# Mixed blocks of four experts in TensorE column groups, in a decoder layer with a mixture of experts

## The chip, the cores and the metric

One core of one Trainium2 chip runs the whole program in one launch. The metric is the device time of that launch in microseconds. The profile is one execution of the same program, taken by the hardware profiler.

## The reference

A decoder layer on 16 sequences of 256 tokens with 256 features, all in float32: self-attention with an altered score function, cross-attention in chunks of 64, and a feed-forward part, each followed by an addition and a layer norm. The change is in the feed-forward part, a mixture of 32 experts with 4 experts per token and a shared expert. Cut to this:

```python
def _L0_ffn_ref(hidden_states, router_weight, router_bias, gate_w, up_w, down_w, shared_gate_w, shared_up_w, shared_down_w):
    tokens = hidden_states.reshape(-1, H)                 # 4096 x 256
    topk_idx, topk_w = _route(tokens, router_weight, router_bias)   # 4 of 32 experts
    gate_vals = jax.nn.silu(jnp.einsum('th,eih->tei', tokens, gate_w))
    up_vals = jnp.einsum('th,eih->tei', tokens, up_w)
    hidden_vals = gate_vals * up_vals                     # 128 wide per expert
    expert_out = jnp.einsum('tei,ehi->teh', hidden_vals, down_w)
    sel = jnp.take_along_axis(expert_out, topk_idx[:, :, None], axis=1)
    mixed = (sel * topk_w[:, :, None].astype(sel.dtype)).sum(1)
    ...
    return mixed + shared
x = _layernorm(x + _L0_ffn_ref(x, L0_ffn_router_weight, L0_ffn_router_bias, L0_ffn_gate_w, L0_ffn_up_w, L0_ffn_down_w, L0_ffn_shared_gate_w, L0_ffn_shared_up_w, L0_ffn_shared_down_w), axis=-1)
```

## The kernel before

The program has three stages. In the first one a loop over the sequences computes both attentions, the router and the shared expert's inner values; GpSimd scatters each token's row (256 features, its routing weight and its address, 258 words) into the DRAM tensor `routed`, in which each expert has a region of its own. That makes 4096 x 4 = 16384 rows. Meanwhile SyncE loads the 32 experts' weights into `w_expert`, where all of them stay.

Then `vec_tables` (L1100) and `pe_tables` (L509) turn the counts of the experts into tables. Each expert has as many blocks of 128 rows as it needs, the last of them partly filled; `shapes` (L45) fixes the number of blocks at the most that any counts can need, (16384 + 32 x 127) // 128 = 159. For each block the tables hold its row address (`tab_i[0]`), the place of its expert's weights in `w_expert` (`tab_i[1]`), and `away`, which sends rows behind an expert's last one to a place where nobody reads. The row addresses are released by the semaphore `v_adr`, the weights' places by `v_tab`.

The second stage, the expert stage, runs over the 159 blocks. In the text a slot is one block's turn. For slot n:

- SyncE loads 128 rows of `routed` into `rowsb` (L1372), 16 buffers deep; from slot 16 on it first waits for the store of slot n - 16 (`st_y`). All loads stand in one queue. After slot 16's it also issues the load of `hs_sb`, 4096 KB, for the last stage (L1375).
- PE transposes the rows (`pe_xbT`, L526, its matmuls are at L284), ScalarE copies the result into `xbT` (L724).
- ScalarE copies the expert's gate and up weights into one of four buffers `wgu` (L857), because a matmul's weights are read from a place that is fixed in the program.
- PE computes gate and up (`pe_gu`, L533 to L540): four matmuls with 128 weight columns from `wgu` and 128 moving columns from `xbT`.
- ScalarE takes the tanh (L853), VectorE makes the inner values `hb` (L1129, L1132).
- PE computes the down projection (`pe_down`, L542 to L546): `hb` as weights, 256 moving columns read from `w_expert` at a register's address.
- VectorE combines it with the routing weight and the row (L1144) into one of four buffers `yb`, so that it waits for the store of slot n - 4, and makes the addresses (L1137); GpSimd scatters the result into the DRAM tensor `y` (L1293).

The order is written out by hand. PE's turn of slot n is transpose for n + 3, gate and up for n + 2, down for n; a float32 matmul shows as two records in the trace. Registers are filled eight at a time by a table load (`values`, L268), one for each eight blocks on PE, ScalarE and SyncE.

The third stage gathers four rows of `y` for each token, adds the shared expert's part on PE and applies the last layer norm (`sync_out` L561 and what follows it). Its code is not touched.

## Time and profile before

| | us |
|---|---|
| median of 3 runs | 827.7 |
| lowest and highest run | 824.57, 830.9 |
| profiled execution, from first to last instruction (span) | 830.3 |
| PE busy | 765.2 |
| VectorE, ScalarE, GpSimd busy | 581.5, 494.4, 368.0 |

The page gives no separate time for the profiled execution. Busy time is a mean over the three stages; the stages lie at about 13 to 503 us, 503 to 764 us and 764 to 830 us of the span. All times in views count from the span's start.

### The profile page before, as it was taken

The numbers are of one execution on the slowest core, as the hardware profiler recorded it, in microseconds if no ns is written. First come the engines' busy times: TensorE is split into PE (matmuls) and PEld (weight loads), VectorE is DVE, ScalarE is ACT, GpSimd is POOL, SyncE is SP. The second block draws the span as 40 slices with busy tenths as digits, with TensorE's granted clock in tenths as the row PEclk, the third lists the DMA queues.
The fourth block names the chain that finished last, engine by engine and source line by source line (L and its number), as shares of the span: only waits on it lengthen the run. The fifth ranks groups of instructions, "written<-read, shape, count | busy, mean of one in ns | idle before, by whom it ended". The sixth has DMA issues, their size and how long they took to land.

```text
span 830.3 us, 21803 instructions
## 1 busy us (share of the span) xinstructions
PE 765.2 (92%) x8308; PEld 665.4 (80%) x8308; DVE 581.5 (70%) x2094; ACT 494.4 (60%) x1166; POOL 368.0 (44%) x437
## 2 busy tenths in 40 slices
PE   7969899999999999999997756799999999999986
PEld 6758788888888888888876636799999999998554
DVE  2345487898889888898888763366666666665486
ACT  0546666767767767777654414467676766764143
POOL 0101214334543355334554662366666666665142
PEclk9999999999999999999989877799999999999999
DMA  6582221332433334332113436755555555552996
GB/s 233 156 214 84 84 84 53 108 118 92 142 121 110 120 99 129 120 110 89 66 65 103 142 111 189 270 172 167 177 172 173 171 169 170 176 168 83 370 401 241
DMA packets 69642, 124.95 MB, mean 150 GB/s; under 512 B 9665, under 2 KB 43329, under 8 KB 69282
## 3 DMA queue, kind: packets, MB, share of 16 engines
q1 hardware_dynamic: 51394, 81.60, 32.1%
q0 software_dynamic: 13776, 37.77, 12.6%
q10 hardware_dynamic: 4368, 4.20, 1.4%
q8 instruction: 66, 1.08, 0.6%
q14 instruction: 38, 0.31, 0.1%
HBM read 73.16 MB, written 50.36 MB: 149 GB/s over the span
## 4 chain that ended last, share of the span: by engine, by line
PE 78%; DMA 7%; DVE 6%; SPq 5%; issue 2%; POOL 1%; ACT 1%; ACTq 0%; DVEq 0%
PE banks L538 17%; PE banks L284 10%; PE banks L545 8%; PE banks L386 3%; PE banks L377 3%; PE banks L354 3%; PE banks L322 3%; PE banks L367 3%; PE banks L489 3%; SPq L567 3%; PE banks L331 3%; PE banks L463 3%; PE banks L498 3%; PE banks L339 3%; DMA w_expert_tile<-y 2%; PE banks L429 2%
## 5 line engine op out<-in xcount | busy, mean ns | idle before, releaser
L1293 POOL DMA_INDIRECT y<-yb_tile,idcol_tile x159 | 152.4, 959 | 112.9 <-DVE yb_tile L1144 110.2
L538 PE MATMUL banks<-xbT_tile,wgu_tile 128*128 128x128 f32 x1272 | 172.0, 280 | 0.0
L538 PEld LDWEIGHTS banks<-xbT_tile,wgu_tile 128*128 128x128 f32 x1272 | 158.6, 196 | 0.1
L1144 DVE SCALAR_TENSOR_TENSOR yb_tile<-banks,rowsb_tile 128x256 f32<-128x256 f32 x159 | 76.9, 484 | 84.2 <-PE banks L545 76.1
L857 ACT ACTIVATE wgu_tile<-w_expert_tile 128x512 f32 x159 | 98.9, 622 | 11.8 <-DVE tab_i_tile L1121 11.8
L545 PE MATMUL banks<-w_expert_tile,hb_tile 128*128 x318 | 96.3, 385 | 5.2 <-DVE hb_tile L1132 5.2
L1271 POOL DMA_INDIRECT routed<-row_tile,idx_tile x64 | 62.5, 976 | 68.8 <-PE banks L399 53.2
L853 ACT ACTIVATE gb_tile<-banks 128x128 f32<-128x128 f32 x159 | 44.1, 277 | 79.1 <-PE banks L538 79.1
L1265 POOL DMA_INDIRECT routed<-row_tile,idx_tile x64 | 61.7, 964 | 31.1 <-issue 18.5
L1246 POOL TENSOR_TENSOR rs_tile<-ve_tile,half_neg_tile 128x2 f32<-128x2 f32 x16 | 11.1, 693 | 143.6 <-DVE ve_tile L960 143.6
L284 PE MATMUL banks<-const_tile,rowsb_tile 128*128 128x128 f32 x318 | 62.2, 278 | 7.1 <-DMA rowsb_tile<-routed 7.1
L724 ACT ACTIVATE xbT_tile<-banks 128x256 f32<-128x256 f32 x159 | 59.7, 376 | 13.2 <-PE banks L284 12.9
L284 PEld LDWEIGHTS banks<-const_tile,rowsb_tile 128*128 128x128 f32 x318 | 45.4, 144 | 23.7 <-DMA rowsb_tile<-routed 7.9
L545 PEld LDWEIGHTS banks<-w_expert_tile,hb_tile 128*128 128x128 f32 x318 | 48.8, 194 | 6.4 <-issue 6.4
L1132 DVE TENSOR_TENSOR hb_tile<-hb_tile,banks 128x128 f32<-128x128 f32 x159 | 45.7, 287 | 5.5
L1241 POOL TENSOR_TENSOR xc_tile<-x_sb_tile,c_out_tile 128x256 f32<-128x256 f32 x32 | 22.7, 734 | 55.9 <-ACT x_tile L816 28.4
L1129 DVE SCALAR_TENSOR_TENSOR hb_tile<-gb_tile,banks 128x128 f32<-128x128 f32 x159 | 44.6, 281 | 3.8 <-ACT gb_tile L853 3.8
L638 ACT ACTIVATE w_expert_tile<-w_expert_tile,fnmr_tile,frs_tile 128x256 f32<-128x256 f32 x32 | 17.6, 593 | 48.5 <-DVE fnmr_tile L618 48.5
L631 POOL TENSOR_TENSOR frs_tile<-fve_tile,fhalf_tile 128x2 f32<-128x2 f32 (+1 forms) x17 | 17.9, 1056 | 42.6 <-DVE fve_tile L613 42.6
L322 PE MATMUL banks<-xT_tile,g_qk_tile 128*128 128x256 f32 x128 | 32.4, 399 | 4.5 <-DMA xT_tile<-xT 4.5
L498 PE MATMUL banks<-x2T_tile,w_shared_in_tile 128*128 128x256 f32 x128 | 33.5, 409 | 1.3 <-ACT sc_tile L836 1.2
L595 PE MATMUL banks<-w_expert_tile,const_tile 128*128 128x512 f32 (+1 forms) x68 | 30.1, 575 | 3.7 <-DMA w_expert_tile<-y 3.6
(206 smaller groups left out, 1784.4 us busy)
## 6 DMA issues: line engine op xcount, KB each, us to landing
rowsb_tile<-routed SPq DMA_DIRECT2D x159, 129.0 KB, 2.2
w_expert_tile<-y SPq DMA_DIRECT2D x15, 1024.0 KB, 15.0
w_expert_tile<-w_expert SPq DMA_DIRECT2D x16, 768.0 KB, 4.6
cT_tile<-ctxT SPq DMA_DIRECT2D x16, 384.0 KB, 3.2
routed<-zrow_tile SPq DMA_DIRECT2D x1, 4128.0 KB, 22.5
xT_tile<-xT SPq DMA_DIRECT2D x16, 256.0 KB, 3.0
x_sb_tile<-x SPq DMA_DIRECT2D x16, 256.0 KB, 2.7
inner<-hs_tile SPq DMA_DIRECT2D x16, 256.0 KB, 2.3
```

Source lines behind the costliest of these rows:

```text
L284: return e.transpose(o, i, ident)
L322: m = e.matmul(bank[5][:, db * S:(db + 1) * S], g_qk[:, k, db * P:(db + 1) * P], xT[:, k, :], start=k == 0, stop=k == DK - 1)
L498: m = e.matmul(bank[7][:, b * S:(b + 1) * S], w_shared_in[:, k, 2 * P + b * P:3 * P + b * P], x2T[i % 2][:, k, :], start=k == 0, stop=k == ...
L538: m = e.matmul(bank[2 + u % 4][:, h * P:(h + 1) * P], wgu[u % WG][:, k * D + h * EI:k * D + (h + 1) * EI], xbT[u % 2][:, k * P:(k + 1) * P ...
L545: e.matmul(bank[6 + u % 2][:, 0:D], hb[u % 4][:, :], w_flat[:, bass.ds(w + 2 * D, D)], start=True, stop=True).then_inc(SEM["p_down"], 1)
L724: e.activation(o, i, ACT.Copy).then_inc(SEM[done], 1)
L857: e.activation(wgu[u % WG][:, :], w_flat[:, bass.ds(w, DK * D)], ACT.Copy)
L1132: e.tensor_tensor(hb[u % 4][:, :], hb1[u % 2][:, :], bank[2 + u % 4][:, EI:2 * EI], ALU.mult)\
L1144: e.scalar_tensor_tensor(yb[n % YS][:, :], bank[6 + u % 2][:, 0:D], rowsb[n % ROWS][:, D:D + 1], rowsb[n % ROWS][:, 0:D], ALU.mult, ALU.ad ...
L1265: e.indirect_dma_start(routed, bass.IndirectOffsetOnAxis(ap=idx[i % 2][:, 0, k:k + 1], axis=0), row[i % 2][:, k, 0, :], None).then_inc(SEM ...
L1271: e.indirect_dma_start(routed, bass.IndirectOffsetOnAxis(ap=idx[i % 2][:, 1, k:k + 1], axis=0), row[i % 2][:, k, 1, :], None).then_inc(SEM ...
L1293: e.indirect_dma_start(y, bass.IndirectOffsetOnAxis(ap=idcol[n % ROWS][:, :], axis=0), yb[n % YS][:, :], None).then_inc(SEM[f"st_y{n % YS} ...
```

## The change

The 16384 rows are exactly 128 full blocks. After the change there are 128 whole slots ("F") and 12 mixed ones ("Q"). A mixed slot has four parts of 32 rows, each of an expert of its own. An expert's remainder, what is left behind its full blocks, is either given a whole slot (`F`) or cut into one to four parts of 32 rows. The tables rank the experts by the number of parts of their remainders, and the largest remainders get the whole slots that are left. `quarters` finds the largest number of parts that any counts can leave, so that 12 mixed slots are enough. `slots` puts one mixed slot behind every ten whole ones and the last eight whole ones at the end.

In a mixed slot the roles of the operands are swapped: `xbT` is the weights, 32 columns for each part, and the experts' weights are the moving operand, 256 columns, each part writing the 32 partitions of its own column group. The inner values come out with the rows on the partitions, so PE transposes `hb` (`pe_hbT`), ScalarE copies it (`act_hbT`), and the down projection is four matmuls again. The weights of the four experts are read from `wq`, which SyncE fills for each mixed slot from DRAM with four DMAs; it is laid over `w_cross` and `w_shared_in`, which are not used any more in this stage. ScalarE's copy into `wgu` falls away for a mixed slot. The rows of a mixed slot come in four loads of 32 rows.

```diff
+QR = P // 4
+LAG = 6
 def shapes(nseq):
     n = nseq * S
-    blocks = (n * TOPK + E * (P - 1)) // P
-    return n, P + n, blocks
+    full = n * TOPK // P
+    groups = -(-quarters(n * TOPK, full) // 8) * 2
+    return n, P + n, full, groups
+def slots(nseq):
+    _, _, full, groups = shapes(nseq)
+    every = full // groups
+    out = []
+    for g in range(groups):
+        out += [("F", g * every + j) for j in range(every)] + [("Q", g)]
+    return out + [("F", j) for j in range(groups * every, full)]
...
-        w_cross = sb("w_cross", [P, DK, 4, D])
+        w_early = sb("w_early", [P, DK * 4 * D + DK * 2 * SH])
+        w_cross = w_early[:, 0:DK * 4 * D].rearrange("p (k j n) -> p k j n", k=DK, j=4)
+        w_shared_in = w_early[:, DK * 4 * D:].rearrange("p (k n) -> p k n", k=DK)
+        wq = w_early[:, :].rearrange("p (q n) -> p q n", q=4)
...
+        def pe_gu(e, s):
+            e.wait_ge(SEM["a_xbT"], s + 1)
+            kind, g = SLOTS[s]
+            o = bank[2 + s % 4]
...
+            if kind == "Q":
+                e.wait_ge(SEM["ld_wq"], 64 * (g + 1))
+            for k in range(DK if kind == "Q" else 0):
+                for q in range(4):
+                    at = k * P + q * QR
+                    m = e.matmul(o[q * QR:(q + 1) * QR, 0:2 * EI], xbT[s % 2][:, at:at + QR],
+                                 wq[:, q, k * D:(k + 1) * D], start=k == 0, stop=k == DK - 1)
             m.then_inc(SEM["p_gu"], 1)
+        def pe_hbT(e, s):
+            e.wait_ge(SEM["v_hb"], s + 1)
+            transpose(e, bank[2 + s % 4][:, 2 * EI:2 * EI + P], hb[s % 4][:, :]).then_inc(SEM["p_hbT"], 1)
+        def pe_down(e, s, w):
...
+                e.wait_ge(SEM["a_hbT"], g + 1)
+                for q in range(4):
+                    m = e.matmul(o[q * QR:(q + 1) * QR, 0:D], hbT[g % 2][:, q * QR:(q + 1) * QR],
+                                 wq[:, q, 2 * D:3 * D], start=True, stop=True)
...
+        def act_hbT(e, s):
+            g = SLOTS[s][1]
+            e.wait_ge(SEM["p_hbT"], g + 1)
+            copy(e, hbT[g % 2][:, :], bank[2 + s % 4][:, 2 * EI:2 * EI + P], "a_hbT")
...
         def vec_tables(e, ch):
-            ch(e.tensor_scalar(cnt_i[:, :], counts[:, :], float(P - 1), None, ALU.add))
+            ch(e.tensor_scalar(cnt_i[:, :], c("round", E), counts[:, 0:1], None, ALU.add))
+            e.tensor_scalar(cnt_i[:, 0:2], cnt_i[:, 0:2], 7, None, ALU.logical_shift_right)
+            ch(e.tensor_scalar(cnt_i[:, 2:3], cnt_i[:, 2:3], 5, None, ALU.logical_shift_right))
...
+            ch(e.tensor_scalar(above[:, :], bank[7][0:E, 8:8 + E], order[:, 0:1], None, ALU.is_gt))
+            ch(e.tensor_reduce(rank[:, :], above[:, :], AX.X, ALU.add))
...
+            def load_wq(g):
+                if g % 2 == 0:
+                    wanted.update(values(mybir.EngineType.SP, 1, FULL + 4 * g))
+                if g > 0:
+                    e.wait_ge(SEM["p_down"], SLOTS.index(("Q", g - 1)) + 1)
+                for q, a in enumerate(quarter(g)):
+                    e.dma_start(wq[:, q, :], d["w_expert"].rearrange("p e n -> p (e n)")[:, bass.ds(wanted.pop(a), 3 * D)])                        .then_inc(SEM["ld_wq"], 16)
...
+            for s, (kind, n) in enumerate(SLOTS):
+                if s >= ROWS:
+                    e.wait_ge(SEM[f"st_y{s % YS}"], 16 * ((s - ROWS) // YS + 1))
...
+                if s >= LAG and SLOTS[s - LAG][0] == "Q":
+                    load_wq(SLOTS[s - LAG][1])
+                if s == ROWS:
                     e.wait_ge(SEM["st_hs"], 16 * nseq)
                     e.dma_start(hs_sb[:, :, :, :].rearrange("p i k s -> p (i k s)"), inner[:, :]).then_inc(SEM["ld_hs"], 16)
```

Two places show what moves. The first is PE, in the slots around a mixed one. Before, every turn reads as these rows do (L284 transposes a slot's rows, L538 is gate and up, L545 the down projection; "waits" names the semaphores):

```order
L284 MATMUL banks<-const_tile,rowsb4_tile 128x128 [waits ld_row4]
L284 MATMUL banks<-const_tile,rowsb4_tile 128x128
L538 MATMUL banks<-xbT1_tile,wgu3_tile 128x128 [waits a_xbT]
L538 MATMUL banks<-xbT1_tile,wgu3_tile 128x128 x3
L545 ISA [waits v_hb]
L545 MATMUL banks<-w_expert_tile,hb1_tile 128x256
```

After the change these stand around the first mixed slot, number 10 (L338 transposes, L600 and L620 are gate and up and down of a whole slot, L607 and L624 those of a mixed one):

```order
L607 MATMUL banks<-w_early_tile,xbT0_tile 32x256 [waits ld_wq,a_xbT]
L607 MATMUL banks<-w_early_tile,xbT0_tile 32x256 x7
L620 ISA [waits v_hb]
L620 MATMUL banks<-w_expert_tile,hb0_tile 128x256
L338 MATMUL banks<-const_tile,rowsb12_tile 128x128 [waits ld_row12]
L338 MATMUL banks<-const_tile,rowsb12_tile 128x128
L600 MATMUL banks<-xbT1_tile,wgu3_tile 128x128 [waits a_xbT]
L600 MATMUL banks<-xbT1_tile,wgu3_tile 128x128 x3
L338 MATMUL banks<-const_tile,hb2_tile 128x128 [waits v_hb]
L620 ISA [waits v_hb]
L620 MATMUL banks<-w_expert_tile,hb1_tile 128x256
```

The four gate and up matmuls of one slot have become eight with a wait for the weights' load, and the transpose of `hb` (hb2 is slot 10's) stands ahead of the down projection of slot 9.

The second place is SyncE's queue. Before, one row load follows the other, each behind the store of the slot 16 before it:

```order
L1372 ISA [waits st_y2]
L1372 DMA rowsb14_tile<-routed 128x258
L1372 ISA [waits st_y3]
L1372 DMA rowsb15_tile<-routed 128x258
L270 TENSOR_LOAD tab_i_tile
L1372 ISA [waits st_y0]
L1372 DMA rowsb0_tile<-routed 128x258
```

After the change the load of slot 27 (rowsb11) is followed by the fetches for the second mixed slot, number 21:

```order
L1489 ISA [waits st_y3]
L1489 DMA rowsb11_tile<-routed 128x258
L1478 REGISTER_ALU [waits p_down]
L1478 DMA w_early_tile<-w_expert 128x768
L1478 REGISTER_ALU
L1478 DMA w_early_tile<-w_expert 128x768
L1478 REGISTER_ALU
L1478 DMA w_early_tile<-w_expert 128x768
L1478 REGISTER_ALU
L1478 DMA w_early_tile<-w_expert 128x768
L1489 ISA [waits st_y0]
```

The fetches stand behind a row load that waits for the store of slot 11, and the next row load stands behind them.

## Rows read from the trace of the kernel before

**Rows 1.** The page: PE in 40 slices of the span, tenths; the DMA packets.
```profile
PE   7969899999999999999997756799999999999986
...
DMA packets 69642, 124.95 MB, mean 150 GB/s; under 512 B 9665, under 2 KB 43329, under 8 KB 69282
```

**Rows 2.** Stretches: length, busy PE, PEld, DVE, ACT, POOL (instructions), PE clock, DMA share, GB/s.
```profile
60.00:430.00 370.00, 361.89 (x5313) 317.24 (x5311) 303.66 (x1022) 260.83 (x568) 149.22 (x199) 1.00 0.31 99
...
545.00:763.00 218.00, 217.37 (x1683) 202.82 (x1682) 146.32 (x565) 148.91 (x418) 135.44 (x142) 1.00 0.55 165
...
532.00:536.00 4.00, 4.00 (x19) 3.71 (x18) 1.90 (x8) 1.56 (x4) 1.72 (x3) 0.50 0.53 177
```

**Rows 3.** Groups by line, 420 to 780 us: busy us, mean ns, idle before.
```profile
L538 PE MATMUL banks<-xbT_tile,wgu_tile 128*128 128x128 f32 x1272 | 172.0, 280 | 0.0
...
L545 PE MATMUL banks<-w_expert_tile,hb_tile 128*128 x318 | 96.3, 385 | 5.2 <-DVE hb_tile L1132 5.2
```

**Rows 4.** Timeline of PE in the steady part: start us, duration us, engine, line.
```profile
559.86 0.60 PE L545 MATMUL banks<-w_expert_tile,hb_tile 128*128 x2
560.29 0.38 PE L284 MATMUL banks<-const_tile,rowsb_tile 128*128 128x128 f32 x2
560.51 1.06 PE L538 MATMUL banks<-xbT_tile,wgu_tile 128*128 128x128 f32 x8
561.40 0.60 PE L545 MATMUL banks<-w_expert_tile,hb_tile 128*128 x2
...
756.18 0.60 PE L545 MATMUL banks<-w_expert_tile,hb_tile 128*128 x2
```

**Rows 5.** Timeline of PE, matmuls in column groups of the attention stage and their successor.
```profile
256.44 0.65 PE L443 MATMUL banks<-sha_tile,vM_tile 128*32 128x64 f32 x32
...
257.36 1.10 PE L455 MATMUL banks<-rden_tile,const_tile 128*32 128x64 f32 x64
258.39 1.99 PE L386 MATMUL banks<-w_expert_tile,w_cross_tile 128*128 128x256 f32 x8
```

**Rows 6.** Timeline of DVE, the same beat as rows 4.
```profile
562.82 0.29 DVE L1132 TENSOR_TENSOR hb_tile<-hb_tile,banks 128x128 f32<-128x128 f32 x1
```

**Rows 7.** Timeline, start of the expert stage: scatter 0, gate and up 4, load 16.
```profile
512.18 0.95 POOL L1293 DMA_INDIRECT y<-yb_tile,idcol_tile  x1 [12.09 <-DVE yb_tile L1144]
...
512.98 1.06 PE L538 MATMUL banks<-xbT_tile,wgu_tile 128*128 128x128 f32 x8
...
514.72 0.33 SPq L1372 DMA_DIRECT2D rowsb_tile<-routed  x1
```

**Rows 8.** Timeline around the load of hs_sb; in brackets the idle time before.
```profile
516.81 0.96 POOL L1293 DMA_INDIRECT y<-yb_tile,idcol_tile  x1 [0.59 <-DVE yb_tile L1144]
...
529.37 0.48 DVE L1144 SCALAR_TENSOR_TENSOR yb_tile<-banks,rowsb_tile 128x256 f32<-128x256 f32 x1 [3.86 <-DMA y<-yb_tile,idcol_tile]
...
530.58 1.22 PE L545 MATMUL banks<-w_expert_tile,hb_tile 128*128 x2 [2.27 <-DVE hb_tile L1132]
```

**Rows 9.** DMA issues: KB each, median us from issue to landing.
```profile
rowsb_tile<-routed SPq DMA_DIRECT2D x159, 129.0 KB, 2.2
...
w_expert_tile<-w_expert SPq DMA_DIRECT2D x16, 768.0 KB, 4.6
...
hs_sb_tile<-inner SPq DMA_DIRECT2D x1, 4096.0 KB, 14.4
```

**Rows 10.** Timeline of SyncE's queue: the first 16 row loads; two of them.
```profile
502.69 8.68 SPq L1372 DMA_DIRECT2D rowsb_tile<-routed  x16
...
507.94 0.85 SPq L1372 DMA_DIRECT2D rowsb_tile<-routed  x2
```

**Rows 11.** Timeline of the tables; the last line is of the chain that ended last.
```profile
490.73 0.20 PE L513 MATMUL banks<-const_tile,macc_tile 128*32 128x1 f32 x2 [1.34 <-DVE hs_tile L1071]
...
496.64 0.24 DVE L1120 TENSOR_SCALAR tab_i_tile<-tab_tile 1x160 int32<-1x160 f32 x1
...
499.13 2.54 DMA routed<-row_tile,idx_tile
```

More of the change, by code:

```diff
@@ L4 @@
 from contextlib import ExitStack
+import functools
 P = 128
@@ L65, in constants @@
         (p[:, None] <= np.arange(E)[None]),
-        np.tile(np.arange(table), (P, 1)),
+        row(np.arange(full), np.arange(4 * groups)),
         p[:, None],
-        n * TOPK + np.arange(blocks)[None, :] * P + p[:, None],
+        p[:, None] % QR,
+        -p[:, None],
+        row([0, P - 1, QR - 1]),
+        n * TOPK + np.arange(full + groups)[None, :] * P + p[:, None],
     ]
     at, out = 0, {}
-    for name, a in zip(("ident", "before", "ones", "headmask", "denmask", "spread", "region", "upto", "blockno", "part", "nowhere"), parts):
+    for name, a in zip(("ident", "before", "ones", "headmask", "denmask", "spread", "region", "upto", "number",
+                        "part", "part32", "minus", "round", "nowhere"), parts):
         out[name] = (at, a.shape[1])
@@ L220, in build @@
         ctx_a.close()
+        place = sb("place", [E, E + 3])
+        over = sb("over", [E, 1])
+        order = sb("order", [E, 1])
+        above = sb("above", [E, E])
+        rank = sb("rank", [E, 1])
+        some = sb("some", [E, 1])
+        rows_full = sb("rows_full", [E, 1])
+        step = sb("step", [1, TABLE])
         past = sb("past", [E, TABLE])
@@ L263, in __call__, with quarter, loads @@
                 self.e.wait_ge(SEM[self.name], self.n)
[L265 to L266 removed]
         def values(engine, row, n):
             _, v = nc.values_load_multi_w_load_instructions(
[L271 removed]
+                tab_i[0:1, row, n:n + UNROLL], engines=[engine], min_val=0,
+                max_val=(E * REGION - (P if n < FULL else QR), (E - 1) * 3 * D)[row],
                 skip_runtime_bounds_check_because="the table is clamped to the experts and their regions for any counts")
             return {n + u: v[u] for u in range(UNROLL)}
+        def quarter(g):
+            return range(FULL + 4 * g, FULL + 4 * g + 4)
+        def loads(s):
+            return sum(64 if SLOTS[a][0] == "Q" else 16 for a in range(s % ROWS, s + 1, ROWS))
         blk = ctx.enter_context(nc.Block())
```

299 lines of the change are left out of this document (170 added, 129 removed).

## The prediction

> **What bounds the kernel now.** I read the page first: TensorE stands at 9 tenths in nearly every slice [rows 1]. The change touches the expert stage, so the stretches come next: from 545 to 763 us PE is busy 217.37 of 218.00 us at a granted clock of 1.00, DVE 146, ACT 149, POOL 135, and the DMA share is 0.55 [rows 2]. The groups by line name the work there: 159 slots, each with 8 records of L538 and 2 of L545 on PE [rows 3], besides two transposes (L284). The timeline shows the beat: the down projections at 559.86 and 756.18 are 127 slots apart, 1.546 us each, and within a slot the transposes (0.22 to the next line), gate and up (0.89) and down (0.44) follow each other without a gap [rows 4]. So a slot costs PE's own time, and a slot removed is worth 1.546 us as long as nothing else takes PE's place.
>
> Two places are different. The stage begins only when the rows are there, and around 520 to 537 the 4096 KB load of hs_sb, which takes 14.4 us [rows 9], holds back the scatters: the one issued at 516.81 lands when the combine at 529.37 starts, PE waits 2.27 us for hb, and the granted clock reads 0.50 [rows 2, 8]. The change keeps this stall, so it is no term of the sum.
>
> **What goes.** 159 slots become 140, in the pattern ten whole, one mixed, twelve times, then eight whole. 19 x 1.546 = 29.4 us of PE time leave the bounding engine. DVE and POOL lose their 19 as well and stay below PE.
>
> **What a mixed slot adds on PE.** Gate and up are 8 matmuls of 32 weight columns by 256 moving columns in four column groups, down is 4 such. Whether four groups run at once, rows show: L443 does 32 matmuls of 32 columns by 64 (64 records) between 256.44 and 257.36, L455 the same number between 257.36 and 258.39 [rows 5]. The steady slot gives the price of moving columns: 0.44 us for the one 256-column matmul of down [rows 4], hence 0.11 per 64 columns, and 32 of these one after the other would take 3.5 us. They took 0.92 and 1.03, 3.8 and 3.4 times less. So the mixed slot's gate and up take about 2 x 0.44 = 0.88 and down 0.44, the same as a whole slot's. Beyond that: (a) the transpose of hb, half of the 0.22 for two, 0.11; (b) entering and leaving the column groups. If the groups ran at a full four times the speed, L455 would take 0.88; it takes 0.15 more and L443 0.04 more; I take 0.18 for each of the two grouped stretches of a mixed slot, 0.36, a little above both, since here each stretch is entered from whole matmuls and left again; (c) the transpose stands ahead of the down projection of the slot before and waits for hb of the mixed slot. In the steady beat hb is written at 562.82 plus 0.29 = 563.11, and the down projection of the slot before begins at 561.40 + 1.546 = 562.95 [rows 4, 6]: 0.16 us of wait, behind which the down projection queues. The ScalarE copy of the transposed hb has a whole slot until down wants it, and ScalarE saves its weight copy for a mixed slot. Sum 0.62, times 12 = 7.4 us. Lower bound 0.11 (all else hidden), upper bound 2.0, if each of the four changes between whole and grouped matmuls cost as much as an isolated matmul lasts (385 ns, L545 in [rows 3]) and the wait is 0.4.
>
> The Trainium skill speaks against the change here. "TensorEngine Tiling (Array Packing)", Key Properties, says that a change of tiling mode drains the array, and "TensorE: Matmul & The Clock Gate", Single matmul latency, gives a constant of 398 cycles at 2.4 GHz; an estimate from the two is 0.17 us a drain, four to a mixed slot, 0.66 where I have 0.36, some 4 us more in all. The rows above hold the two lines L443 and L455 behind each other without that.
>
> **What a mixed slot adds on the queues.** Its weights are fetched from DRAM for each mixed slot: four DMAs of 384 KB into w_early, 1536 KB, 12 times. SP issues them behind the row load of six slots later, which itself waits for the store of the slot ten before the mixed one. So their time is short and can be counted. In the trace the row load number 16 goes out at 514.72, when store 0 has landed; the gate-and-up matmuls of slot 4 start at 512.98, so those of slot 10, the first mixed one, would start at 512.98 + 6 x 1.546 = 522.26 [rows 7]. That leaves 7.5 us. All later groups repeat this: the same ten slots stand between. Against it: 0.52 us for the row load (two in 0.85 with 0.33 for the last), and a table load for every second group. Its price: 16 row loads took 8.68 us, 15 x 0.52 + 0.33 = 8.13, the rest, 0.55, is the one table load; 0.28 on average [rows 7, 10]. The transfer: 129 KB land in 2.2 us and 768 KB in 4.6 us [rows 9], 3.76 ns more per KB, so 1536 KB land 2.2 + 1407 x 0.00376 = 7.5 us after the first issue. Together 8.3 us, 0.8 us too late. PE then stands at the mixed slot's gate and up, and down, scatter and combine of the slots behind queue up: the whole 0.8 us is lost, 12 x 0.8 = 9.6 us. Bounds: the 4096 KB load needs (14.4 - 2.2) / 3967 = 3.1 ns per KB, landing in 6.5 us, no wait; and if the scatters' half of the 0.55 DMA share [rows 2] comes on top of that price, it is 2.2 + 5.3 / 0.73 = 9.5 us, a wait of 2.8. I take 0.8, because the 768 KB loads were timed beside traffic of 0.31 DMA share (60 to 430 us in [rows 2]), about what the scatters make.
>
> Do the fetches hold back the scatters as hs_sb does? A combine comes 4 slots, 6.2 us, after the one whose store it waits for. A scatter issued at 512.18 has landed at 514.72, 2.5 us [rows 7], and the combine itself is 0.48 [rows 8]. That leaves about 3 us. The hs_sb load is made of large packets (only 360 of the 69642 are 8 KB or more [rows 1]), these of 3 KB: if each of a scatter's 1 KB packets stands behind one of 3 KB, it moves four times the bytes of its own, and a landing grows by some 1.2 us. Hidden. The row loads queued behind a fetch are wanted ten slots later. The first fetch comes ahead of hs_sb, and the hs_sb stall moves back with it; I keep its size.
>
> **The tables.** Between PE's L513 (490.73) and v_adr (L1120, 496.64 + 0.24) 15 DVE operations turn into 29, with a fourth hand-over to PE and three more matmuls. The 15 with three hand-overs took 6.15 us, 0.41 each, so 14 more take at most 5.7; at the 0.24 that L1120 itself takes they are 3.4. I take 4, since most of the new ones are one column wide, so v_adr comes near 500.9. The row loads wait for the last scatter anyway, issued at 499.13 and landed 2.54 later at 501.67 [rows 11]. Cost 0, at most 0.9 by the first price. Table loads on PE and ScalarE stand between other waits and cost nothing now; ScalarE's now precede the copy that uses them, and ScalarE, busy 149 of 218 us, waits for gate and up in every slot, which covers that.
>
> **Sum.** 29.4 - 7.4 - 9.6 - 0 = 12.4 us less. The profiled execution's span is 830.3 us; the page states no separate time for it, and the span is 2.6 above the median of the runs shown (827.7) and within their 824.57 to 830.9. From 830.3 it goes to 817.9, and against the median to 815.3, which I predict.
>
> **The rivals.**
> A, the fetches are in time. Speaks for it: the 4096 KB load's 3.1 ns per KB. Against: the 3.76 of the smaller ones. 29.4 - 7.4 = 22.0, 805.7 us.
> B, the other side: the fetch is the bound of every group. Place: PE before the mixed slot's gate and up. Break-even is a wait of (29.4 - 7.4) / 12 = 1.8 us; from there the kernel is slower. At 2.8 us it is 33.6 + 7.4 - 29.4 = 11.6 slower, 839.3 us. For it: the scatters share the engines, and PE's wait stands in each group anew. If the wait reaches the 2.3 us of [rows 8], the half clock beside it can follow too; four us at 0.50, as one window there shows [rows 2], lose 2 us more in each group, 24 in all. Against it: the price of 9.5 us for a fetch charges the scatters twice, as said above.
> C, the column groups don't overlap with 256 moving columns: 12 matmuls x 0.44 instead of 3 x 0.44, 4.0 us a mixed slot, 48 us, 863 us. For it: nothing in the trace has 256 columns in a group. Against: L443 and L455, with four different moving operands and with one.
> The Trainium skill ("TensorE: Matmul & The Clock Gate", Measured speedup vs the span model) gives 3.07 for four row tiles and 2.38 for three column tiles; by the first, an estimate, 1.32 us of grouped work become 1.72, 4.8 us in all, still the forecast's case.
>
> **How the numbers follow.** Forecast (wait 0.3 to 1.6) 0.45; A 0.25; B 0.22; C 0.08. Low end: A with mixed slots at 0.4 instead of 0.62, 803. High end: B, 839. More than 1% (8.3 us, about what a measurement of this kernel can tell from no change) faster: A, and the forecast up to a wait of 1.1, 0.28: 0.53. Slower by over 1%: C, and B from a wait of 2.5, 0.14: 0.22. The rest, 0.25, is within 1%.
>
> **What would show it.** A whole slot stays at 1.546; a mixed slot without its wait is 0.6 longer; PE's idle time before the grouped matmuls of gate and up, released by the w_early DMA, is near 0.8 times 12; the four fetches land 7.5 us after the first issue; the granted clock stays 1.00 between 545 us and the end of the stage; the first row load stays near 502.7. Wrong would be a wait of nothing or above 1.8, combines waiting for stores at every group, or grouped records that follow each other 0.44 us apart.

## The result

The changed kernel takes 837.17 us, median of 5 runs (834.13 to 841.48), against 828.52 (824.57 to 831.67) for the kernel before on the same chip: a ratio of 1.0107 with a 95% interval of 1.0068 to 1.0145. Two later controls with both kernels unaltered, where the kernel before is as fast, gave 833.71 against 827.20 and 833.22 against 827.64. The prediction was 815.3, faster; the kernel is about 1% slower. The value lies in the stated range of 803 to 839. A slower kernel was given 30 chances in 100 (rivals B and C), one slower by over 1% 22. The ratios leave out executions in a slower state of the chip: none here, three in the experiments (842.21, 1000.2 and 4368.72 us).

The profiled execution has a span of 834.7 us and a time of 836.51.

This is the page of the kernel after, to be held against [rows 1]: PE in 40 slices of the span, the granted clock of PE (TensorE) in tenths, the DMA packets.

```profile
PE   7879999999999999999987638989898889799987
...
PEclk9989999999999999999999769999999999999999
...
DMA packets 73482, 138.83 MB, mean 166 GB/s; under 512 B 10401, under 2 KB 41633, under 8 KB 73122
```

PE's slices of the expert stage alternate between 8 and 9 where they all stood at 9: something recurs. Here are the windows of the kernel after, with the columns of [rows 2]:

```profile
506.00:545.00 39.00, 31.55 (x236) 27.25 (x234) 19.48 (x76) 20.28 (x56) 18.21 (x19) 0.96 0.88 317
545.00:763.00 218.00, 196.29 (x1567) 167.22 (x1568) 119.91 (x464) 126.57 (x350) 110.68 (x116) 0.98 0.66 210
577.84:586.34 8.50, 6.55 (x51) 5.93 (x50) 5.16 (x20) 4.79 (x14) 4.49 (x6) 1.00 0.91 301
```

From 545 to 763 us PE is busy 196.29 us where it was 217.37. It has less to do, as meant, but the 21 us are now idle time inside the stage. The groups by line of the kernel after say what it waits for (busy us, mean ns, idle time before and its releaser; they answer to [rows 3]):

```profile
L600 PE MATMUL banks<-xbT_tile,wgu_tile 128*128 128x128 f32 x1024 | 137.8, 278 | 0.0
...
L620 PE MATMUL banks<-w_expert_tile,hb_tile 128*128 x256 | 80.4, 397 | 1.9 <-DVE hb_tile L1238 1.9
...
L607 PE MATMUL banks<-w_early_tile,xbT_tile 128*32 128x256 f32 x192 | 15.5, 445 | 27.3 <-DMA w_early_tile<-w_expert 27.3
...
L1251 DVE SCALAR_TENSOR_TENSOR yb_tile<-banks,rowsb_tile 128x256 f32<-128x256 f32 x140 | 67.7, 484 | 114.6 <-PE banks L620 86.3 <-DMA y<-yb_tile,idcol_tile 20.8 <-PE banks L624 7.6
```

The first matmul of the mixed slots' gate and up waits 27.3 us in all for the weights, 2.27 for each of the 12; the forecast was 9.6 in all, 0.8 for each. And the combines wait 20.8 us in all for a store, where the kernel before has 8.1.

This is the timeline of PE around one mixed slot in the kernel after (it answers to [rows 4]):

```profile
582.03 0.60 PE L620 MATMUL banks<-w_expert_tile,hb_tile 128*128 x2
...
583.57 0.60 PE L620 MATMUL banks<-w_expert_tile,hb_tile 128*128 x2
584.01 0.38 PE L338 MATMUL banks<-const_tile,rowsb_tile 128*128 128x128 f32 x2
586.34 1.07 PE L607 MATMUL banks<-w_early_tile,xbT_tile 128*32 128x256 f32 x16 [1.96 <-DMA w_early_tile<-w_expert]
587.35 0.70 PE L620 MATMUL banks<-w_expert_tile,hb_tile 128*128 x2
587.88 0.38 PE L338 MATMUL banks<-const_tile,rowsb_tile 128*128 128x128 f32 x2
588.10 1.06 PE L600 MATMUL banks<-xbT_tile,wgu_tile 128*128 128x128 f32 x8
589.21 0.33 PE L338 MATMUL banks<-const_tile,hb_tile 128*128 128x128 f32 x1
589.37 0.62 PE L620 MATMUL banks<-w_expert_tile,hb_tile 128*128 x2
589.83 0.38 PE L338 MATMUL banks<-const_tile,rowsb_tile 128*128 128x128 f32 x2
590.05 1.06 PE L600 MATMUL banks<-xbT_tile,wgu_tile 128*128 128x128 f32 x8
591.04 0.64 PE L624 MATMUL banks<-w_early_tile,hbT_tile 128*32 128x256 f32 x8
```

The whole slots are still 1.54 us apart (582.03, 583.57). The 16 records of L607 with 256 moving columns take 1.07 us to their last end and 1.01 to the next line. One after the other they would take eight times 0.44 us: the four column groups do run at once. These are SyncE's queue in the same stretch, and the landing of the last of the four fetches, from the chain that ended last:

```profile
577.28 0.34 SPq L1489 DMA_DIRECT2D rowsb_tile<-routed  x1
577.84 2.21 SPq L1478 DMA_DIRECT2D w_early_tile<-w_expert  x4
```

```profile
579.71 6.50 DMA w_early_tile<-w_expert
```

The row load that the fetch stands behind goes out at 577.28, the first fetch at 577.84, the last lands at 586.21. The third window above is just this stretch: the 16 DMA engines are busy 0.91 of the time and move 301 GB/s. The DMA issues of the kernel after are these (KB each, median us from issue to landing; they answer to [rows 9]):

```profile
w_early_tile<-w_expert SPq DMA_DIRECT2D x48, 384.0 KB, 5.1
rowsb_tile<-routed SPq DMA_DIRECT2D x128, 129.0 KB, 2.6
...
hs_sb_tile<-inner SPq DMA_DIRECT2D x1, 4096.0 KB, 18.3
...
y<-yb_tile,idcol_tile POOLq DMA_INDIRECT x140, 3.3
```

A store lands after 3.3 us at the median, where it took 2.5 in the kernel before. Beside a fetch it is worse. These are a scatter and a combine of the kernel after, around the fetch issued at 619.24:

```profile
619.26 0.96 POOL L1398 DMA_INDIRECT y<-yb_tile,idcol_tile  x1 [0.59 <-DVE yb_tile L1251]
```

```profile
626.15 0.48 DVE L1251 SCALAR_TENSOR_TENSOR yb_tile<-banks,rowsb_tile 128x256 f32<-128x256 f32 x1 [1.95 <-DMA y<-yb_tile,idcol_tile]
```

The combines between them start at 620.05, 621.59 and 623.14. So the one at 626.15 is the fourth behind the one whose scatter went out at 619.26, and takes the same `yb` buffer: that scatter took 6.9 us until its buffer was used again.

### The profile page after: what moved, and what is told of

The parts are those of the page before. It is cut to its first block, busy times and chain, and to the rows that moved or that the text cites. A ratio compares the mean times of both kernels' runs of the same rounds, so it can differ in the third digit from the quotient of the medians.

```text
span 834.7 us, 21727 instructions
## 1 busy us (share of the span) xinstructions
PE 745.9 (89%) x8274; PEld 629.4 (75%) x8274; DVE 564.1 (68%) x2036; ACT 475.6 (57%) x1109; POOL 349.7 (42%) x418
## 4 chain that ended last, share of the span: by engine, by line
PE 62%; DMA 19%; DVE 8%; SPq 6%; issue 3%; POOL 1%; ACT 1%; ACTq 0%; DVEq 0%
DMA w_early_tile<-w_expert 8%; PE banks L338 8%; DMA y<-yb_tile,idcol_tile 6%; PE banks L600 5%; PE banks L440 3%; PE banks L431 3%; PE banks L408 3%; PE banks L376 3%; PE banks L421 3%; PE banks L620 3%; PE banks L543 3%; PE banks L385 3%; PE banks L517 3%; PE banks L552 3%; PE banks L393 3%
## 5 line engine op out<-in xcount | busy, mean ns | idle before, releaser
L1398 POOL DMA_INDIRECT y<-yb_tile,idcol_tile x140 | 134.1, 958 | 141.1 <-DVE yb_tile L1251 138.6
L1251 DVE SCALAR_TENSOR_TENSOR yb_tile<-banks,rowsb_tile 128x256 f32<-128x256 f32 x140 | 67.7, 484 | 114.6 <-PE banks L620 86.3
L600 PE MATMUL banks<-xbT_tile,wgu_tile 128*128 128x128 f32 x1024 | 137.8, 278 | 0.0
L600 PEld LDWEIGHTS banks<-xbT_tile,wgu_tile 128*128 128x128 f32 x1024 | 127.4, 196 | 0.2
L944 ACT ACTIVATE wgu_tile<-w_expert_tile 128x512 f32 x128 | 79.8, 623 | 22.4 <-DVE tab_i_tile L1226 15.6
L620 PE MATMUL banks<-w_expert_tile,hb_tile 128*128 x256 | 80.4, 397 | 1.9 <-DVE hb_tile L1238 1.9
L805 ACT ACTIVATE xbT_tile<-banks 128x256 f32<-128x256 f32 x140 | 52.7, 377 | 14.0 <-PE banks L338 11.9
L338 PE MATMUL banks<-const_tile,rowsb_tile 128*128 128x128 f32 x280 | 56.0, 283 | 3.3 <-DMA rowsb_tile<-routed 3.2
L338 PEld LDWEIGHTS banks<-const_tile,rowsb_tile 128*128 128x128 f32 x280 | 39.0, 145 | 22.9 <-issue 7.1
L620 PEld LDWEIGHTS banks<-w_expert_tile,hb_tile 128*128 128x128 f32 x256 | 39.5, 195 | 9.3 <-issue 9.3
L607 PE MATMUL banks<-w_early_tile,xbT_tile 128*32 128x256 f32 x192 | 15.5, 445 | 27.3 <-DMA w_early_tile<-w_expert 27.3
```

Source lines behind the costliest of these rows:

```text
L338: return e.transpose(o, i, ident)
L600: m = e.matmul(o[:, h * P:(h + 1) * P], wgu[s % WG][:, k * D + h * EI:k * D + (h + 1) * EI], xbT[s % 2][:, k * P:(k + 1) * P], start=k == ...
L620: m = e.matmul(o[:, 0:D], hb[s % 4][:, :], w_flat[:, bass.ds(w.pop(g) + 2 * D, D)], start=True, stop=True)
L805: e.activation(o, i, ACT.Copy).then_inc(SEM[done], 1)
L944: e.activation(wgu[s % WG][:, :], w_flat[:, bass.ds(w.pop(n), DK * D)], ACT.Copy)
L1251: e.scalar_tensor_tensor(yb[s % YS][:, :], bank[6 + s % 2][:, 0:D], rowsb[s % ROWS][:, D:D + 1], rowsb[s % ROWS][:, 0:D], ALU.mult, ALU.ad ...
```

## The experiments

There are three theories. **L**, lateness: each fetch lands too late and PE's wait stands in full; the cure is to start the fetch earlier. **S**, the fetches hold the scatters back, so the combines run late; the cure is more `yb` buffers or less traffic. **M**, the mixed slot itself costs PE more than thought. Sixteen runs in four groups test them, each group beside the kernel before on its own chip. The chips are of two kinds: on those of groups 1 and 3 the kernel before takes 870 and 871 us instead of 828, so only ratios are compared between the two kinds. A ratio with its interval is not the quotient of the two medians, and can differ from it by up to 0.5%.

`LAG` is the number of slots by which a fetch's place in SyncE's queue lies behind the mixed slot's own row load. A smaller one is an earlier fetch. Below 6, the first fetch needs a wait of its own for the tables, in all these kernels:

```diff
-LAG = 6
+LAG = 5        # 4 in other runs
...
+                if g == 0:
+                    e.wait_ge(SEM["v_tab"], 1)
```

**Group 1 (kernel before 870.12 us).**

Fetch one slot earlier:

> The changed kernel with the fetches for a mixed slot issued one slot earlier (LAG 5; SyncE also waits for v_tab before the first). Theory L (lateness): the loss is PE's wait for fetches that go out too late; the wait falls from 27 us in all to 8 to 12, and the time by about 16 to 20 us from the changed kernel's 837, so 817 to 821. Rival S (stores): the 18 MB of fetches hold back the scatters, and what PE no longer waits for the fetch it waits through the combines; the time stays above 830 and the combines' wait for stores grows above 25 us.

Measured 846.26 us, 0.9709 (0.9682 to 0.9737). The fetch waits are gone, a mean of 0.06 us for each mixed slot, where 8 to 12 us in all were expected to stay. The combines wait 26.2 us for stores, as S expects, and the kernel is faster all the same.

Fetch two slots earlier:

> The changed kernel with the fetches two slots earlier (LAG 4), as early as the buffer of the mixed slot before is free. Theory L: PE waits for a fetch less than 3 us in all, 808 to 814 us, the granted clock is 1.00 after 545 us. Rival S: combines wait more than 25 us for stores, 825 us or more. Theory M (mixed slots themselves cost much more than 0.62 us over a whole one): the waits are gone and the time is still near 825, with PE busy.

Measured 843.84 us, 0.9686 (0.9665 to 0.9707), no fetch waits; the combines wait 24.9 us for stores.

Only the first fetch is issued, and all mixed slots use its weights, so eleven fetches are left out. `LAG` stays 6:

```diff
-                e.wait_ge(SEM["ld_wq"], 64 * (g + 1))
+                e.wait_ge(SEM["ld_wq"], 64)
...
-                if s >= LAG and SLOTS[s - LAG][0] == "Q":
+                if s >= LAG and SLOTS[s - LAG] == ("Q", 0):
```

> The changed kernel with the fetch for the first mixed slot only; the 11 others use the same weights again, so the output of the experts' remainders is left wrong, and 16.5 MB of traffic are left out. What remains is the price of 140 slots: with 0.9 us for a mixed slot over a whole one 29.4 - 10.8 = 18.6 us below before, and up to 5 more for a shorter stall at the load of hs_sb: 804 to 811 us. Against the kernel with LAG 4: L expects a difference below 4 us, S above 10 us.

Measured 839.35 us, 0.9646 (0.9630 to 0.9662). Against LAG = 4 the combines' waits for stores fall from 24.9 to 6.3 us, and the time by 4.5 us, although this kernel still waits 2.9 us for its one fetch. That lies between what L (below 4) and S (above 10) expected: fetches that arrive early still cost something, but little.

Six `yb` buffers, paid for with four of the sixteen row buffers, and fetches as early as the queue allows:

```diff
-ROWS = 16
-YS = 4
+ROWS = 12
+YS = 6
...
-LAG = 6
+LAG = 0
```

> Fetches as early as with LAG 4, but six buffers yb instead of four and twelve row buffers instead of sixteen (LAG 0 puts the fetch behind the same store). A combine waits for the store six slots back. L: as LAG 4 except for the stall at the load of hs_sb, 3 us shorter for the two more slots of slack, 805 to 811 us. S: more than 10 us below LAG 4, and combines no longer wait for stores outside 510 to 540 us.

Measured 849.75 us, 0.9757 (0.9741 to 0.9773). No combine waits for a store, yet it is 6 us slower than LAG = 4 alone. PE waits for rows instead, 13.7 us, 9.9 of them in one piece; LAG = 4 has 2.0. I read this as twelve row buffers being too few to cover the 4096 KB load of `hs_sb`. What the store waits of the combines cost is less than what these buffers cost.

All four ratios are better than the forecast's own (815.3 of 827.7, 0.985), and the changed kernel had not run on such a chip. So group 2 has the controls.

**Group 2 (kernel before 827.39 us).** These are the controls, both kernels unaltered:

> The kernel before, unchanged, as a control: the chip of the last four runs gave 870 us for it where the first gave 828. Ratio 1.00. If the chip is the slow one again, its profile shows where the 42 us lie. Theory S for that chip: scatters land later than the 6.2 us that four buffers allow, combines wait for stores in most slots, and a whole slot takes about 1.7 us or more. Rival: the attention stage is longer and the slot stays 1.546.

> The changed kernel, unchanged, as a control on the same chip. On a chip where before takes 828: 837. On one where it takes 870: theory L expects it 25 to 30 us above the kernel with LAG 4 (0.969 of before), so a ratio of 0.995 to 1.005; S expects no more than 5 us above it.

Measured 827.20 (1.0009, 0.9978 to 1.0040) and 833.71 (1.0074, 1.0040 to 1.0109). The result holds; the fetch waits are 20.6 us.

The kernel before with six `yb` and twelve row buffers:

> The kernel before with six buffers yb and twelve row buffers in place of four and sixteen. Where stores land in time (828 us chip) only the stall at the load of hs_sb gets shorter, by about 3 us. If S explains the slow chip, the slot falls back to 1.546 there and the time by 20 us or more; if not, it stays within 5.

Measured 831.22, 1.0029 (1.0000 to 1.0058): no gain for the kernel before either. PE's waits for rows grow from 7.1 to 13.7 us there.

LAG = 4, and the load of `hs_sb` divided into 16 of 256 KB, one behind every fourth row load:

```diff
-                    e.dma_start(hs_sb[:, :, :, :].rearrange("p i k s -> p (i k s)"), inner[:, :]).then_inc(SEM["ld_hs"], 16)
+                if ROWS <= s < ROWS + 4 * nseq and s % 4 == 0:
+                    i = (s - ROWS) // 4
+                    e.dma_start(hs_sb[:, i, :, :].rearrange("p k s -> p (k s)"), inner[:, i * DK * S:(i + 1) * DK * S])\
+                        .then_inc(SEM["ld_hs"], 16)
```

> LAG 4, and the 4096 KB load of hs_sb in 16 parts of 256 KB, one for every fourth slot. L: as LAG 4 without the stall, 4 to 8 us below it. S: the fetches of 3 KB a row, which stay, hold the combines back as before, and the gain is only that stall's. Where before takes 828: 803 to 810 us.

Measured 806.69 us (806.17 to 808.11), 0.9745 (0.9692 to 0.9798). This beats both kernels. But it has two steps in one.

**Group 3 (kernel before 871.19 us)** is on a chip of the other kind again:

> The kernel with LAG 4 alone once more, since the chip of its first run gave 870 us for before. On a chip where before takes 827: L expects the changed kernel's 20.6 to 27 us of waits for fetches to go, 808 to 814 us. S expects 820 or more.

> The kernel before with only the load of hs_sb in 16 parts of 256 KB, one every fourth slot. Its trace loses 8.9 us at the load in one piece; if the large packets of one piece are what holds the scatters, 818 to 820 us and no combine waits for a store. If it is the 4096 KB as such, the wait is spread and the time stays at 827. It tells how much of the gain of LAG 4 with the divided load (0.9745 of before) belongs to the change of blocks at all.

> LAG 4 with the divided load of hs_sb and only the first fetch; the other 11 mixed slots use the first one's weights, so the output of the remainders is left wrong and 16.5 MB are not fetched. L: the fetches are hidden once they are early; within 2 us of the kernel with all of them, 805 to 808 us. S: the 28.9 us of combine waits go and with them 5 us or more, 796 to 802 us.

> All fetches, divided load of hs_sb, six buffers yb and twelve row buffers with the fetch behind the same store (LAG 0). S: the slack of two more slots takes up the late stores, as if nothing were fetched: 796 to 802 us, and less than 5 us of combine waits. L: no change against four buffers, 805 to 808 us.

Measured: LAG = 4 alone 844.97, 0.9712 (0.9685 to 0.9738); the kernel before with the divided load 864.59, 0.9937 (0.9905 to 0.9970); LAG = 4, divided load and one fetch only 837.82, 0.9616 (0.9587 to 0.9646); the kernel with six `yb` and twelve row buffers and the divided load 841.67, 0.9660 (0.9631 to 0.9690). LAG = 4 repeats its ratio of group 1. The window of the kernel before with the divided load shows why these chips are not used for the sums: this kernel has neither fetches nor the undivided load, and yet PE is idle 12 of 200 us.

```profile
545.00:745.00 200.00, 188.11 (x1394) 168.59 (x1394) 117.02 (x466) 122.28 (x351) 111.56 (x116) 1.00 0.57 173
```

The timeline shows where. A whole slot still takes 1.546 us on this chip, but 41 of 155 take some 0.5 us more or longer, mostly every third one, at the first matmul of gate and up (two such places; "issue" means that the profile names nothing that PE waits for):

```profile
582.75 1.16 PE L538 MATMUL banks<-xbT_tile,wgu_tile 128*128 128x128 f32 x8 [0.23 <-issue]
...
587.88 1.16 PE L538 MATMUL banks<-xbT_tile,wgu_tile 128*128 128x128 f32 x8 [0.23 <-issue]
```

From 525.40 to 789.64 us the mean slot is 1.70 us. On the other chip the same kernel has no slot above 1.6.

**Group 4 (kernel before 827.64 us)** parts the two steps. (The third text below says "four of 1 MB"; it is the division in 16 shown above.)

> The changed kernel unaltered, as the control of this group; it has not yet been measured on a chip where the kernel before takes 870 us. Theory L (the fetches of the mixed slots land late, and each wait stands in full): 1.007 to 1.011 of the kernel before where that takes 828 us, 833 to 837 us; where it takes 870 us, an unaltered kernel must lie above the same kernel with earlier fetches (0.969 to 0.971) by 12 to 20 us, 856 to 864 us. Theory S (only the late scatters cost): no more than 5 us above the kernel with earlier fetches.

> The change with the fetches two slots earlier (LAG = 4) and nothing else. Where the kernel before takes 828 us: by theory L the waits at the first matmuls on w_early_tile, 20 to 27 us in two profiles, go nearly whole and give 15 to 22 us: 812 to 819 us, with the undivided load of hs_sb still to pay. By theory S at most 5 us are gained: 829 us or more. Where it takes 870 us: 0.969 to 0.971 of it, as in two earlier runs.

> The kernel before with the load of hs_sb divided into four of 1 MB, and nothing else: the share of that step in the version with both steps. Where the kernel before takes 828 us: the waits of that stretch in its profile are 8 to 9 us of TensorE at full or half clock; 819 to 823 us if the division removes them, 827 if not. If it gives 5 to 9 us, the earlier fetches alone are worth 18 to 22 of the 27 us that both steps gave (theory L); if it gave over 15, the fetches would be worth less than half of it. Where it takes 870 us: 0.994.

> The version with both steps (LAG = 4, divided hs_sb load) with only the first of the twelve fetches issued: the later eleven mixed slots use the first one's weights, which leaves the loading of eleven sets of expert weights out. It prices what the traffic of 16.9 MB still costs when no slot waits for it. Theory S (the fetches hold back rows and scatters): 6 us or more under the version with both steps, 800 us or less where the kernel before takes 828 us. Theory L (nothing but lateness): within 3 us of it, 804 to 808 us. Where it takes 870 us: 0.962, as before.

| | us | ratio (95%) | stage | fetch waits |
|---|---|---|---|---|
| before (control, group 2) | 827.20 | 1.0009 (0.9978 to 1.0040) | 262.8 | |
| after (group 4) | 833.22 | 1.0115 (1.0064 to 1.0167) | 267.9 | 23.1 |
| after, LAG = 4 | 814.93 | 0.9856 (0.9827 to 0.9885) | 247.7 | 0.2 |
| before, divided load | 819.60 | 0.9908 (0.9868 to 0.9948) | 253.8 | |
| after, LAG = 4, divided load (group 2) | 806.69 | 0.9745 (0.9692 to 0.9798) | 242.4 | 1.9 |
| the same, one fetch only | 803.33 | 0.9734 (0.9697 to 0.9771) | 238.3 | 1.3 |

"Stage" is the time in the profile from the first row load's issue to the end of the last scatter's record. The stage's start differs by up to 5 us from one execution to the next with the same code ahead of it (502.69 and 498.40 in two profiles of the kernel before), so stages are compared rather than spans.

Starting the fetch earlier, alone, is worth 18.3 us (833.22 to 814.93; 21 by the ratios); L expected 15 to 22. The divided load alone is worth 8.0 in the kernel before. Together they give 27.0 in group 2 (833.71 to 806.69), about the sum. S as the main cause falls: it allowed the earlier fetch at most 5 us. The groups by line of the kernel with LAG = 4 alone show both sides of this:

```profile
L607 PE MATMUL banks<-w_early_tile,xbT_tile 128*32 128x256 f32 x192 | 12.9, 385 | 0.2 <-DMA w_early_tile<-w_expert 0.2
...
L1251 DVE SCALAR_TENSOR_TENSOR yb_tile<-banks,rowsb_tile 128x256 f32<-128x256 f32 x140 | 67.7, 483 | 90.3 <-PE banks L620 53.8 <-DMA y<-yb_tile,idcol_tile 26.7 <-PE banks L624 9.5
```

And its windows, PE busy 198.53 of 200 us at full clock:

```profile
506.00:545.00 39.00, 33.32 (x241) 29.50 (x240) 17.70 (x68) 20.36 (x57) 14.75 (x16) 0.88 0.88 311
545.00:745.00 200.00, 198.53 (x1611) 169.12 (x1610) 124.22 (x484) 130.38 (x360) 115.99 (x122) 1.00 0.74 234
```

PE's wait is gone, while VectorE's waits for stores have not shrunk at all (26.7 us). They cost little (3 to 4 us, below). The likely reason is that VectorE has time to spare and PE's transposes and gate and up run two to three slots ahead of the combine. An idle time named in the profile is only a price if the bounding engine is behind it. Most of what is left of PE's loss lies in the first window: the `hs_sb` stall, at a granted clock of 0.88. With the divided load in the kernel before, the same window reads:

```profile
506.00:545.00 39.00, 39.00 (x305) 36.42 (x303) 25.94 (x101) 27.11 (x77) 23.88 (x25) 1.00 0.68 208
```

The kernel with one fetch only gives the clean price of a mixed slot, theory M. PE's starts of the mixed slots' gate and up, three of twelve:

```profile
592.23 1.07 PE L607 MATMUL banks<-w_early_tile,xbT_tile 128*32 128x256 f32 x16
610.23 1.07 PE L607 MATMUL banks<-w_early_tile,xbT_tile 128*32 128x256 f32 x16
628.23 1.07 PE L607 MATMUL banks<-w_early_tile,xbT_tile 128*32 128x256 f32 x16
```

A group of eleven slots takes 18.00 us (three of the eleven groups 18.16), where eleven whole slots take 11 x 1.546 = 17.01: a mixed slot costs 1.00 us more than a whole one, 1.04 on average, 12.5 us for twelve.

With these numbers I add up the stage, from the 262.8 us of the kernel before:

| | 19 slots | 12 mixed | fetch waits | sum | measured |
|---|---|---|---|---|---|
| after (the result's profile) | -29.4 | +12.5 | +27.3 | 273.2 | 272.7 |
| after (group 2) | -29.4 | +12.5 | +20.6 | 266.5 | 267.1 |
| after (group 4) | -29.4 | +12.5 | +23.1 | 269.0 | 267.9 |
| LAG = 4 | -29.4 | +12.5 | +0.2 | 246.1 | 247.7 |
| one fetch, from the 253.8 of the divided load | -29.4 | +12.5 | +1.3 | 238.2 | 238.3 |
| LAG = 4, divided load, from 253.8 | -29.4 | +12.5 | +1.9 | 238.8 | 242.4 |

The row of the one fetch closes in part by construction, since the 12.5 was read in that profile. Only the last row misses by more than 2 us. Its 3.6 us are what the fetches' traffic costs where hardly anything waits for a fetch itself: the one kernel without that traffic (803.33 against 806.69 us) lacks them. That is S's share, 3 to 4 us. It rests on one profile each and on medians of different groups; by the two ratios (0.9745, 0.9734) it is 1 us, and their intervals overlap.

In the rows of the changed kernel two things cancel, and their timelines show both. The first is the `hs_sb` stall. In the kernel before the down projections at 521.60 and 536.67 are four turns apart and 8.9 us further than 4 x 1.546. In the kernel after the same stretch is this, seven turns:

```profile
516.66 0.60 PE L620 MATMUL banks<-w_expert_tile,hb_tile 128*128 x2
...
535.04 0.60 PE L620 MATMUL banks<-w_expert_tile,hb_tile 128*128 x2
```

18.38 us less 7 x 1.546, one mixed slot's 1.0 and the first fetch wait of 3.23 leave 3.3 us for the stall; the two controls of the changed kernel have 4.9 and 3.2. So 4 to 6 us of the stall are gone. The second is the rest. Counted from the kernel without the stall (253.8 - 29.4 + 12.5 = 236.9), the three stages of 272.7, 267.1 and 267.9 leave 5.2, 4.7 and 4.7 us beyond the fetch waits and the stall: the traffic's share again, and the matmuls at half clock (last section). How these 5 us divide between the two was not tested.

## Why the prediction was wrong

**The 29.4 us that go: right.** Whole slots stay at 1.546 us and the last table closes with 19 of them.

**The step that failed: "8.3 us, 0.8 us too late", 12 x 0.8 = 9.6.** Place and mechanism were as said: PE stands before L607, released by the w_early DMA, at each group. The size was 27.3 us in the result's profile, 20.6 and 23.1 in two more, 1.7 to 2.3 us per group. With the 27.3 us, 17.7 more than forecast, that alone turns the sign of the forecast 12.4; with the 20.6 it takes it to about nothing, and the mixed slots, below, do the rest. In the three profiles (36 groups) L607 starts 7.3 to 9.8 us after the first issue, with a mean of 8.3, where I had 7.5 (my own 8.3 was these 7.5 and 0.8 for the row load and the table load). Without the wait it would have started 6.3 us after that issue, where I had 7.5 less 0.8, 6.7. So the transfer was 0.8 us dearer, the lead 0.4 shorter, and 0.8 + 0.8 + 0.4 = 2.0 is the mean wait of the three.

That the transfer was dearer I put down to its neighbours, without a run that shows it alone: I priced it by loads beside a DMA share of 0.31, and here the engines were 0.91 busy at 301 GB/s. 301 GB/s over 8.5 us are 2.56 MB, of which the fetch is 1.57, so 1 MB of rows and scatters went through with it. My upper bound had charged this (9.5 us). The truth lay between it and my choice, and I had argued the bound down.

The lead was shorter because of the store that starts a fetch: the row load ahead of the fetch waits for it. I took its landing from the first scatter of the stage, 2.54 us [rows 7]. In the kernel after the chain reads so (a scatter, the row load that waited for it, the fetch):

```profile
594.17 0.96 POOL L1398 DMA_INDIRECT y<-yb_tile,idcol_tile  x1 [0.70 <-DVE yb_tile L1251]
```

```profile
596.77 0.33 SPq L1489 DMA_DIRECT2D rowsb_tile<-routed  x1
598.05 1.93 SPq L1478 DMA_DIRECT2D w_early_tile<-w_expert  x4
```

Here it is 2.60 us; over the 36 groups it is 2.98 on average, which is the 0.4. But little of that is the change's doing. In the kernel before, from slot 20 on, a row load goes out 2.54 to 4.47 us after the scatter that it waits for, 2.88 on average: I had taken the quickest case for the usual one. Nor does a fetch stand beside the store that starts the next one. That store goes out about 8 us after the fetch before it has landed (594.17 against 586.21).

**"Hidden": wrong as a reading, harmless as a cost.** Stores land after 3.3 us at the median instead of 2.5, and one that goes out with a fetch took 6.9, where I had reckoned 1.2 us more. So combines do wait for stores, 20.8 us in all. The kernel with LAG = 4 has more of these waits (26.7) and is 18.3 us faster. The Trainium skill ("DMA: Bandwidth & Descriptors", Queues, rings and completion order) has each DMA engine take turns between its queues a whole packet at a time, several descriptors in one. The trace agrees in direction (2.5 to 3.3 us at the median); no run here shows the size of a turn.

**The mixed slot: 0.62 forecast, 1.00 to 1.04 measured**, 5 us over the twelve, the second term of the sum that failed. Held against the beat of [rows 4], the rows of the mixed slot above show where it is: the transpose of `hb` 0.16 and the wait ahead of it 0.22 (588.10 to 589.21 is 1.11 instead of 0.89), forecast 0.11 and 0.16; the remaining 0.64 comes in pieces of 0.03 to 0.14 at and just behind each of the four changes between whole and grouped matmuls (582.03 to 583.57 has none of them). So my 0.36 for the column groups was 0.28 too low. The rule of the Trainium skill that I had set aside ("TensorEngine Tiling (Array Packing)", Key Properties, with the constant of "TensorE: Matmul & The Clock Gate", Single matmul latency) made it 0.66, as an estimate, and the measured 0.64 sides with it; that the pieces are drains no run shows.

**The break-even of rival B** was set at a wait of 1.8 us. With the mixed slot's true price it is (29.4 - 12.5) / 12 = 1.4. All three profiles lie above it (1.7, 1.9, 2.3). By this B was the case that came true; it had 22 chances in 100. "Against it: the price of 9.5 us for a fetch charges the scatters twice" is the sentence that kept it low. That its 839.3 us lie so near the measured 837.17 is in part luck: its wait was too long (33.6 against 27.3 us) and its mixed slots too cheap (7.4 against 12.5).

**The `hs_sb` stall, kept at its size: it shrank**, from 8.9 us to 3.2 to 4.9, as counted above; why is not shown. The sum did not feel it, since the rest of some 5 us, for which the prediction had no term, came in its place. The stall's size could be read from the kernel before: dividing the load gets 8 us there.

**The tables: right.** These are, in the kernel after, PE's first matmul for them and the DVE operation that releases the row addresses, then the landing of the last scatter (compare [rows 11]):

```profile
485.86 0.20 PE L567 MATMUL banks<-const_tile,macc_tile 128*32 128x1 f32 x2 [1.54 <-DVE hs_tile L1156]
...
495.36 0.24 DVE L1225 TENSOR_SCALAR tab_i_tile<-tab_tile 1x176 int32<-1x176 f32 x1
```

```profile
494.25 2.46 DMA routed<-row_tile,idx_tile
```

The tables take 9.7 us where they took 6.15, 3.6 more (forecast 4), and still end ahead of the last scatter's landing at 496.71. Cost 0.

**The column groups: right**, four at once, so rival C fell. **The clock: wrong in part.** It was to stay at 1.00 from 545 us on and is 0.98.

Had the two mis-sized terms been right, the sum would have been -29.4 + 12.5 + 24 (the mean of the three profiles) = 7 us slower; measured were 8.7 by the medians of the result and 5.6 and 6.5 in the controls. The kernel with LAG = 4 takes 814.93 us, the forecast's 815.3 by number but not by its terms: it has no fetch wait (forecast 9.6) and dearer mixed slots (12.5 against 7.4). A fetch two slots earlier is all that the change lacked.

Open: why the same change gains more on the slower chips (LAG = 4: 0.969 and 0.971 there, 0.986 here). One part can be read: the mean slot of the kernel before with the divided load is 1.70 us there instead of 1.546, so 19 slots are worth 3 us more. That is a small part of the 13 us by which the gains differ (26 against 13). What causes the stop at every third slot is not known, and the unaltered changed kernel was not run there.

## What to carry to other kernels

A transfer whose lead you can count must be priced at the upper bound, beside the traffic that fills the engines at that moment, and its start from the mean of many such events, not from one; if the queue order gives two more slots of lead for one constant, take them before anything is measured. Read an engine's waits only where the bounding engine stands behind them: 29 us of VectorE's waits for stores cost some 3 to 4, 23 us of PE's waits for weights cost 18. Price a new kind of step by the period of the group it stands in, with each change between whole and grouped matmuls counted at 0.16 us (0.64 for four here).

## What the runs showed of the hardware

A wait of PE can cost more than itself. In the three profiles of the changed kernel none of the 28 waits of up to 2.52 us is followed by slow matmuls (L607 lasts 1.07 us). Of the eight from 2.54 on, six are followed by an L607 of 1.77 to 1.94 us, one by 1.25, and one, of 3.13, by 1.07. Two neighbours in the kernel after, and the window of the first, at a granted clock of 0.70:

```profile
606.95 1.94 PE L607 MATMUL banks<-w_early_tile,xbT_tile 128*32 128x256 f32 x16 [2.54 <-DMA w_early_tile<-w_expert]
628.79 1.07 PE L607 MATMUL banks<-w_early_tile,xbT_tile 128*32 128x256 f32 x16 [2.38 <-DMA w_early_tile<-w_expert]
```

```profile
604.60:610.00 5.40, 3.05 (x19) 1.58 (x20) 0.83 (x4) 1.06 (x3) 0.96 (x1) 0.70 0.59 202
```

An L607 at half the clock (1.2 instead of 2.4 GHz) alone is 0.87 us more, in a group that had already lost 2.5.

One load of 4096 KB beside small loads and scatters cost 8 us (827.6 to 819.6) that the same bytes in 16 loads, spread over the stage, do not cost; from 506 to 545 us the mean DMA share is 0.72 with the one load and 0.68 with the sixteen. And the same kernel before takes 828 us on one chip and 871 on another. With the divided load, the form of it that has a profile on the slower chip, the granted clock from 545 to 745 us is 1.00 there too; the time goes in stops of some 0.5 us at about every third slot.
